# Group-norm attention on one core: GpSimd and VectorE add all eight probability tiles of a head pair, and TensorE counts once

## The chip, the cores and the metric

One core of one Trainium2 chip runs the whole program. The time is the device time of one execution in microseconds (us). The engines are called as in the profile: PE is TensorE, DVE VectorE, ACT ScalarE, POOL GpSimd, SP SyncE, whose queue issues all DMAs here.

## The reference

The input x has shape (16, 192, 32, 32), so 16 images with 192 channels and 1024 positions, all float32. With `_gn` a group norm over 32 groups of 6 channels:

```
xt  = gn(x) as (16, 1024, 192)
qkv = xt @ qkv_w.T                      # 6 heads of 32 channels
attn = softmax((q @ k.T) * 32 ** -0.5)  # 1024 x 1024 for each head
out = (attn @ v) @ proj_w.T + proj_b
x + out
```

## The kernel before, in words

The program runs in steps, one for each image (`b`), and each step in 24 slots (`s`). A slot is one head pair (`PAIRS` = 3) and one tile of 128 keys (`TILES` = 8). Each slot has four units (`u`): two heads of the pair times two halves of 512 queries. The order of everything is written out by hand. Each engine's block has a function `step` that walks through the slots and units, and lists of slots say where the side work stands. Engines wait for each other through counting semaphores. `run_steps` writes out steps -3 to 0, then a loop whose body is two steps, then the last ones. Steps 0 to 15 attend; the earlier ones only prepare.

In a slot, for each unit, PE multiplies keys and queries into a bank of `scores_ps` (L528, two banks), and ACT takes the exponential from there into `probs` (L671), a ring of four tiles. After the second score, PE weighs the slot before: `weigh` (L543) accumulates v times probabilities into `heads_ps`, four column groups, 32 rows each. In parallel PE works on the row maxima of 12 slots later (`row_max`, L453) in three banks of `max_ps`, and DVE reduces them (L812). They become the shift rows, two further rows of `q_stack`.

The denominator of the softmax: POOL adds probability tiles in pairs (L738, two adds of 128x1024 in each odd slot), and PE sums each pair over its 128 keys with a matrix of ones (`count`, L558), which accumulates in `sums_ps`: four counts for each head pair, so 12 a step. ACT copies the sums (L646), SP spreads them, DVE takes the reciprocal (L884), SP writes them through memory and broadcasts them (L394, L397), POOL multiplies the heads (L715) and splits off a low half (L720), and SP moves both halves to `attn_a_hi` and its like (L411).

The side work on PE shares one bank, `extra_ps`, which is freed through `extra_freed`: the products for q and k (`QK_SLOTS`, `QK_LATE_SLOTS`), for v (`V_SLOTS`), the projection (`PROJ_SLOTS`), the transposes for the shift rows (`SHIFT_SLOTS`), the group's mean and variance. q and k are split into a high half by ACT (L601) and a low half by DVE (L865). SP then stacks them with 18 DMAs a step in slots 7, 9 and 11 (`stack_pair`, L359). In slot 13 ACT waits for all of these before it writes `qk_hi` for the next image.

DVE also takes the batch norm statistics in slots 16 and 17 and adds the projection to the residual (L858). The residual `x_res` gets its bias from POOL in slot 9 (L727). POOL computes rstd in slot 2 (L690) and the low halves of the normalised x in slots 8 and 10 (L697, L706).

## Time and profile before

| | us |
|---|---|
| median of the runs (1839.04 to 1847.8) | 1840.49 |
| the profiled execution | 1852.48 |
| its span, first to last instruction | 1850.7 |
| PE busy | 1685.4 |
| ACT busy | 1209.1 |
| DVE busy | 1197.5 |
| POOL busy | 1193.3 |

Busy time counts an engine's instructions, overlaps once. The durations of matmuls overlap, so what one costs in a row of them is read from the distance of the starts. The mean granted clock of PE is 0.951 of 2.4 GHz: it lies at 2.4 GHz with short stretches at 1.2 GHz.

### The profile page before, as it was taken

How to read it: one execution, taken by the hardware profiler on the slowest of the kernel's cores; microseconds unless marked ns; L12 is line 12 of the kernel's file. 1: busy time of each engine (PE TensorE's matmuls, PEld its weight loads, DVE VectorE, ACT ScalarE, POOL GpSimd, SP SyncE). 2: the span in 40 equal slices, each digit the busy share in tenths (PEclk: the TensorE clock that was granted, in tenths of full speed). 3: DMA queues.
4: the chain of work that ended last, by engine and by line, in shares of the span. 5: the costliest groups of instructions: out<-in, count | busy, mean ns of one | idle time of the engine just before them, and what ended most of it. 6: DMA issues, size and time to landing. Idle time of an engine off the chain costs nothing.

```text
span 1850.7 us, 30248 instructions
## 1 busy us (share of the span) xinstructions
PE 1685.4 (91%) x9440; PEld 546.9 (30%) x9440; DVE 1197.5 (65%) x2086; ACT 1209.1 (65%) x1969; POOL 1193.3 (64%) x581
## 2 busy tenths in 40 slices
...
GB/s 68 74 1 81 30 87 42 91 26 54 92 47 87 14 70 75 47 93 48 75 31 71 75 48 87 31 88 39 49 97 48 87 13 84 38 70 53 58 14 80
DMA packets 74284, 109.27 MB, mean 59 GB/s; under 512 B 26176, under 2 KB 39040, under 8 KB 74112
## 3 DMA queue, kind: packets, MB, share of 16 engines
...
q14 instruction: 83, 0.68, 0.1%
...
## 4 chain that ended last, share of the span: by engine, by line
PE 69%; DMA 10%; SPq 9%; ACT 4%; issue 3%; DVE 2%; POOL 1%; ACTq 0%; POOLq 0%; DVEq 0%
PE heads_ps L543 16%; PE max_ps L453 16%; PE scores_ps L528 15%; PE sums_ps L558 9%; SPq L359 7%; DMA k_stack<-qk_lo 7%; ACT probs L671 3%; PE extra_ps L511 2%; DMA inv_rows<-inv_spread 2%; PE extra_ps L512 2%; PE extra_ps L513 2%; PE extra_ps L515 2%; PE extra_ps L516 2%; PE extra_ps L475 1%; PE extra_ps L474 1%
## 5 line engine op out<-in xcount | busy, mean ns | idle before, releaser
L812 DVE TENSOR_REDUCE half_max<-max_ps 128x1 f32<-128x512 f32 x1536 | 1014.8, 686 | 437.6 <-PE max_ps L453 401.9
L671 ACT ACTIVATE probs<-scores_ps,exp_scale 128x512 f32<-128x512 f32 x1536 | 995.8, 688 | 436.7 <-PE scores_ps L528 409.2
L738 POOL TENSOR_TENSOR prob_pairs<-probs 128x1024 f32<-128x1024 f32 x384 | 898.1, 2357 | 511.3 <-ACT probs L671 510.5
L528 PE MATMUL scores_ps<-q_stack,k_stack 98*128 98x512 f16 x1536 | 600.3, 392 | 84.8 <-ACT probs L671 65.8
L453 PE MATMUL max_ps<-k_stack,q_stack 96*128 96x512 f16 x1536 | 607.4, 397 | 7.1 <-DVE half_max L812 4.7
L543 PE MATMUL heads_ps<-probs,v_sb 128*32 128x512 f32 x3072 | 417.4, 616 | 0.1
L453 PEld LDWEIGHTS max_ps<-k_stack,q_stack 96*128 96x128 f16 x1536 | 151.7, 99 | 597.2 <-issue 492.1
L528 PEld LDWEIGHTS scores_ps<-q_stack,k_stack 98*128 98x128 f16 x1536 | 151.8, 99 | 264.6 <-ACT probs L671 181.1
L558 PE MATMUL sums_ps<-prob_pairs,ones 128*32 128x512 f32 x1536 | 215.3, 634 | 1.1 <-POOL prob_pairs L738 1.1
L865 DVE TENSOR_TENSOR qk_lo<-extra_ps,qk_hi 128x512 f16<-128x512 f32 x96 | 66.1, 688 | 107.6 <-ACT qk_hi L601 107.6
L601 ACT CAST qk_hi<-extra_ps 128x512 f16<-128x512 f32 x96 | 55.8, 581 | 95.8 <-DMA k_stack<-qk_lo 58.4
L543 PEld LDWEIGHTS heads_ps<-probs,v_sb 128*32 128x32 f32 x3072 | 60.9, 109 | 144.5 <-issue 133.7
L727 POOL TENSOR_SCALAR x_res<-x_res,bias 96x1024 f32<-96x1024 f32 x32 | 90.7, 2845 | 5.0 <-DMA x_res<-x 4.6
L858 DVE SCALAR_TENSOR_TENSOR x_res<-extra_ps,proj_unscale,x_res 96x512 f32<-96x512 f32 x64 | 46.1, 720 | 48.9 <-PE extra_ps L516 48.9
L626 ACT ACTIVATE xhat<-x_sb,neg_mu_rstd,rstd 128x512 f32<-128x512 f32 x64 | 51.2, 806 | 40.1 <-POOL neg_mu_rstd L693 40.1
L690 POOL TENSOR_TENSOR rstd<-var_eps,minus_half 128x2 f32<-128x2 f32 x16 | 11.5, 716 | 92.3 <-DVE var_eps L849 92.3
L715 POOL TENSOR_TENSOR heads_out<-heads_sb,inv_sb 128x512 f32<-128x512 f32 x48 | 60.8, 1266 | 4.6 <-POOL xhat_b L706 3.5
L720 POOL TENSOR_TENSOR heads_lo<-heads_out,heads_hi 128x512 f16<-128x512 f32 x48 | 55.5, 1156 | 12.1 <-ACT heads_hi L614 12.1
L558 PEld LDWEIGHTS sums_ps<-prob_pairs,ones 128*32 128x32 f32 x1536 | 30.9, 110 | 78.6 <-issue 72.7
L511 PE MATMUL extra_ps<-xhat_a_hi,w_hi 128*128 128x512 f16 x96 | 38.2, 398 | 17.2 <-POOL xhat_b L706 9.4
L614 ACT CAST heads_hi<-heads_out 128x512 f16<-128x512 f32 x48 | 29.6, 617 | 32.3 <-POOL heads_out L715 32.3
L511 PE MATMUL extra_ps<-attn_a_hi,wp_hi 128*96 128x512 f16 x64 | 25.4, 397 | 22.9 <-DMA attn_b<-heads_lo 20.3
...
## 6 DMA issues: line engine op xcount, KB each, us to landing
...
```

What stands on the lines that cost most here:

```text
L359: sp.dma_start(stack[D * n:D * (n + 1), par, 2 * p:2 * p + 2, :], part[row % P:row % P + 2 * D, row // P, :]).then_inc(stacked[p], MOVE)
L453: pe.matmul(max_ps[:, bank, :], q_stack[0:STACK, par, h, P * tile:P * (tile + 1)], k_stack[0:STACK, par, h, HALF * half:HALF * (half + 1)] ...
L511: pe.matmul(to, hi[:, 0, :], a_hi, start=True, stop=False)
L528: pe.matmul(scores_ps[:, u_bank(s, u), :], k_stack[0:SHIFTED, st.parity, h, P * tile:P * (tile + 1)], q_stack[0:SHIFTED, st.parity, h, HAL ...
L543: last = pe.matmul(heads_ps[at:at + D, :], v_sb[:, par, tile, D * h:D * (h + 1)], probs[:, a, s % RING, HALF * half:HALF * (half + 1)], st ...
L558: last = pe.matmul(sums_ps[at:at + D, :], ones[:, 0:D], prob_pairs[:, a, q % PAIR_RING, HALF * half:HALF * (half + 1)], start=(at_pair == ...
L671: nc.scalar.activation(probs[:, a, s % RING, HALF * half:HALF * (half + 1)], scores_ps[:, u_bank(s, u), :], ACT.Exp, scale=exp_scale[:, 0: ...
L715: nc.gpsimd.tensor_tensor(heads_out[:, :], heads_sb[:, (par + p) % 2, :], inv_sb[:, :], ALU.mult).then_inc(divided, 1)
L727: nc.gpsimd.tensor_scalar(x_res[:, t, :], x_res[:, t, :], bias[:, t:t + 1], None, ALU.add).then_inc(res_biased, 1)
L738: nc.gpsimd.tensor_tensor(prob_pairs[:, a, j % PAIR_RING, :], probs[:, a, (s - 1) % RING, :], probs[:, a, s % RING, :], ALU.add).then_inc( ...
L812: nc.vector.tensor_reduce(half_max[:, a, tile, half:half + 1], max_ps[:, bank, :], AX_X, ALU.max).then_inc(max_read[bank], 1)
L865: nc.vector.tensor_tensor(qk_lo[:, t, n], extra_ps[:, :], qk_hi[:, t, n], ALU.subtract).then_inc(extra_freed, 1)
```

## The change

The banks: `sums_ps` is gone and `scores_ps` has a third bank. The exponentials of units 0 to 2 go to `probs`, now a ring of six tiles with 1536 columns. Those of unit 3 go to `probs_last`, eight tiles with 512 columns.

The sums: POOL no longer adds in pairs. In each slot but the first of a head pair it adds the tile to `prob_sums`, in two instructions of 1024 and 512 columns. DVE sums unit 3: in slots 4 and 8 after a pair's start, after units 1 and 3, it reduces four tiles at a time over 256 columns (`sum_quads`). The first four go into `prob_sums`, the second four into `quad_sums`. POOL adds these two at the next pair's first slot. PE then sums each pair once over its keys, into `extra_ps`, in slots 10, 18 and 2 of the next step (`SUMS_SLOTS`). ACT copies it out at the next slot's start.

The bias of the residual moves from POOL to ACT, in slots 10 and 11. Mean and variance go from slots 0 and 2 to 0 and 1, with rstd in slot 2 still. One q and k product goes from slot 16 to 15, two projections from 17 and 18 to 16 and 17. Spreading, reciprocal, broadcasting, dividing, and moving the heads of pairs 1 and 2 stand one slot earlier.

```diff
-SCORE_BANKS = 2
+SCORE_BANKS = 3
 MAX_BANKS = 3
 MAX_UNITS = SCORE_UNITS * SLOTS // MAX_BANKS
-RING = 4
-PAIR_RING = 4
+RING = 6
+QUAD = 4
+WIDE = 3 * HALF
+ADDED = 2 * (TILES - 1) + 1
+QUADS = 4
...
-MEAN_SLOT, VAR_SLOT = 0, 2
+MEAN_SLOT, VAR_SLOT = 0, 1
+RSTD_SLOT = 2
...
-QK_SLOTS = (12, 16, 19)
+QK_SLOTS = (12, 15, 19)
 QK_LATE_SLOTS = (3, 4, 6)
-PROJ_SLOTS = (17, 18, 20, 22)
-EXTRA_SLOTS = (*SHIFT_SLOTS, MEAN_SLOT, VAR_SLOT, *V_SLOTS, *QK_SLOTS, *QK_LATE_SLOTS, *PROJ_SLOTS)
+PROJ_SLOTS = (16, 17, 20, 22)
+SUMS_SLOTS = {10: 0, 18: 1, 2: 2}
...
-BIAS_SLOT = 9
+BIAS_AT = ((10, 1), (11, 3))
...
 HEADS_TAKEN = TILES
-SUMS_TAKEN = TILES + 4
-SUMS_SPREAD = TILES + 5
-INVERTED = TILES + 6
-INV_SPREAD = TILES + 7
-DIVIDED = TILES + 11
-MOVED = (23, 22, 22)
-COUNT_UNIT, HEADS_UNIT, SUMS_UNIT = 3, 2, 3
+SUMS_SPREAD = TILES + 4
+INVERTED = TILES + 5
+INV_SPREAD = TILES + 6
+DIVIDED = TILES + 10
+MOVED = (23, 21, 21)
+HEADS_UNIT = 2
...
-        sums_ps = psum("sums_ps", [P, HALF])
...
-        probs = sb("probs", [P, 2, RING, N], F32)
-        prob_pairs = sb("prob_pairs", [P, 2, PAIR_RING, N], F32)
+        probs = sb("probs", [P, RING, WIDE], F32)
+        probs_last = sb("probs_last", [P, 2 * QUAD, HALF], F32)
+        prob_sums = sb("prob_sums", [P, 2, 2 * N], F32)
+        quad_sums = sb("quad_sums", [P, HALF], F32)
...
-                        sp.wait_ge(sums_taken, k + 1)
+                        sp.wait_ge(extra_freed, st.ordinal(s - 2) + 1)
...
+                elif kind == "sums" and part == 0:
+                    j, par = st.summed(i)
+                    pe.wait_ge(tiles_added, ADDED * (PAIRS * j + i + 1))
+                    for half in range(HALVES):
+                        for a in range(2):
+                            at, u = D * (2 * half + a), 2 * a + half
+                            last = pe.matmul(extra_ps[at:at + D, :], ones[:, 0:D],
+                                             prob_sums[:, (par + i) % 2, HALF * u:HALF * (u + 1)],
+                                             start=True, stop=True)
...
-            def count(b, q):
-                p, at_pair = divmod(q, PAIRS_A_HEAD)
-                pe.wait_ge(pairs_added, 2 * (SLOTS // PAIR * b + q + 1))
-                if at_pair == 0 and due(PAIRS * b + p):
-                    pe.wait_ge(sums_taken, PAIRS * b + p)
-                for half in range(HALVES):
-                    for a in range(2):
-                        at = D * (2 * half + a)
-                        last = pe.matmul(sums_ps[at:at + D, :], ones[:, 0:D],
-                                         prob_pairs[:, a, q % PAIR_RING, HALF * half:HALF * (half + 1)],
-                                         start=(at_pair == 0), stop=(at_pair == PAIRS_A_HEAD - 1))
-                last.then_inc(sums_done, 1)
...
+                elif kind == "sums":
+                    k = PAIRS * st.summed(i)[0] + i
+                    if due(k):
+                        act.wait_ge(sums_spread_out, MOVE * k)
+                    nc.scalar.copy(sums_sb[:, :], extra_ps[:, :]).then_inc(extra_freed, 1)
+            def add_bias(st, t):
+                if t == 0:
+                    act.wait_ge(res_loaded, MOVE * st.b)
+                nc.scalar.activation(x_res[:, t, :], x_res[:, t, :], ACT.Identity,
+                                     bias=bias[:, t:t + 1]).then_inc(res_biased, 1)
...
+                                was, tile = divmod(s - RING, TILES)
                                 act.wait_ge(heads_done, SLOTS * st.b + s - RING + 1)
-                                act.wait_ge(pairs_added, 2 * (SLOTS // 2 * st.b + (s - RING) // 2 + 1))
+                                act.wait_ge(tiles_added, ADDED * (PAIRS * st.b + was) + 2 * max(tile, 1))
+                            k = PAIRS * st.b + s // TILES
+                            if u == 3 and s % QUAD == 0 and due(k):
+                                act.wait_ge(quads_summed, QUADS * (k - 1) + 2 * (s % TILES // QUAD + 1))
...
-                    if st.tail and s == BIAS_SLOT:
-                        pool.wait_ge(res_loaded, MOVE * st.b)
-                        pool.sem_inc(res_seen, 1)
-                        for t in range(2):
-                            nc.gpsimd.tensor_scalar(x_res[:, t, :], x_res[:, t, :], bias[:, t:t + 1], None,
-                                                    ALU.add).then_inc(res_biased, 1)
-                    if st.attend and s % 2 == 1:
-                        j = s // 2
-                        for a in range(2):
-                            pool.wait_ge(probs_ready, SCORE_UNITS * (SLOTS * st.b + s) + 2 * (a + 1))
-                            counted = SLOTS // PAIR * st.b + j - PAIR_RING + 1
-                            if a == 0 and due(counted):
-                                pool.wait_ge(sums_done, counted)
-                            nc.gpsimd.tensor_tensor(prob_pairs[:, a, j % PAIR_RING, :],
-                                                    probs[:, a, (s - 1) % RING, :],
-                                                    probs[:, a, s % RING, :], ALU.add).then_inc(pairs_added, 1)
+                    for j, par, p in st.due(s, TILES, TILES):
+                        k = PAIRS * j + p
+                        last = prob_sums[:, (par + p) % 2, WIDE:WIDE + HALF]
+                        pool.wait_ge(quads_summed, QUADS * (k + 1))
+                        nc.gpsimd.tensor_tensor(last, last, quad_sums[:, :], ALU.add).then_inc(tiles_added, 1)
+                    if st.attend and s % TILES != 0:
+                        p, tile = divmod(s, TILES)
+                        k = PAIRS * st.b + p
+                        for n, cols in enumerate((slice(0, N), slice(N, WIDE))):
+                            to = prob_sums[:, (st.parity + p) % 2, cols]
+                            pool.wait_ge(probs_ready, SCORE_UNITS * (SLOTS * st.b + s) + n + 2)
+                            if tile == 1:
+                                if n == 0 and due(k - 1):
+                                    pool.wait_ge(extra_filled, st.ordinal(TILES * p))
+                                before = probs[:, (s - 1) % RING, cols]
+                            else:
+                                pool.wait_ge(tiles_added, ADDED * k + 2 * (tile - 2) + n + 1)
+                                before = to
+                            nc.gpsimd.tensor_tensor(to, before, probs[:, s % RING, cols],
+                                                    ALU.add).then_inc(tiles_added, 1)
...
+            def sum_quads(st, s, u):
+                for g in range(2):
+                    for j, par, p in st.due(s, QUAD * (g + 1), TILES):
+                        k = PAIRS * j + p
+                        n = slice(N // 4 * (u // 2), N // 4 * (u // 2 + 1))
+                        if u == 1:
+                            dve.wait_ge(probs_ready, SCORE_UNITS * (SLOTS * j + TILES * p + QUAD * (g + 1)))
+                            if g == 0 and due(k - 1):
+                                dve.wait_ge(extra_filled, st.ordinal(TILES * p))
+                            if g == 1 and due(k):
+                                dve.wait_ge(tiles_added, ADDED * k)
+                        to = quad_sums[:, n] if g == 1 else prob_sums[:, (par + p) % 2, WIDE:WIDE + HALF][:, n]
+                        nc.vector.tensor_reduce(to, probs_last[:, QUAD * g:QUAD * (g + 1), n].rearrange("p t n -> p n t"),
+                                                AX_X, ALU.add).then_inc(quads_summed, 1)
...
+def tile_of(probs, probs_last, s, u):
+    return probs_last[:, s % (2 * QUAD), :] if u == 3 else probs[:, s % RING, HALF * u:HALF * (u + 1)]
```

On POOL, in the loop, from slot 8 of a step on, before the change. `prob_pairs` takes two tiles, and two adds stand for each two slots:

```order
L696 REGISTER_ALU
L697 TENSOR_TENSOR xhat_a_lo<-xhat,xhat_a_hi 128x1024 [waits xhat_ready]
L724 REGISTER_ALU
L727 TENSOR_SCALAR x_res<-x_res,bias 96x1024 [waits res_loaded]
L727 TENSOR_SCALAR x_res<-x_res,bias 96x1024
L733 ISA
L737 REGISTER_ALU [waits probs_ready]
L738 TENSOR_TENSOR prob_pairs<-probs 128x1024 [waits sums_done]
L733 REGISTER_ALU
L738 TENSOR_TENSOR prob_pairs<-probs 128x1024 [waits probs_ready]
```

The same engine and place after the change. `prob_sums` is the running sum, L735 the last add of a pair, and L751 the add of a tile, here the first of a pair:

```order
L703 REGISTER_ALU
L704 TENSOR_TENSOR xhat_a_lo<-xhat,xhat_a_hi 128x1024 [waits xhat_ready]
L734 ISA
L735 TENSOR_TENSOR prob_sums<-prob_sums,quad_sums 128x512 [waits quads_summed]
L742 ISA
L746 REGISTER_ALU [waits probs_ready]
L751 TENSOR_TENSOR prob_sums<-probs 128x1024 [waits extra_filled]
L742 REGISTER_ALU
L751 TENSOR_TENSOR prob_sums<-probs 128x512 [waits probs_ready]
```

The bias is gone from between the low half of x-hat and the adds, and in its place stands the last add, which waits for DVE's `quads_summed`.

On DVE, in the loop, slot 16 before the change, with two of the four statistics (`half_stats`):

```order
L812 TENSOR_REDUCE half_max<-max_ps 128x1 [waits max_filled1]
L788 ISA
L789 BN_STATS half_stats<-x_sb 128x6 [waits x_loaded]
L812 TENSOR_REDUCE half_max<-max_ps 128x1 [waits max_filled2]
L808 REGISTER_ALU
L812 TENSOR_REDUCE half_max<-max_ps 128x1 [waits max_filled0]
L789 BN_STATS half_stats<-x_sb 128x6
L812 TENSOR_REDUCE half_max<-max_ps 128x1 [waits max_filled1]
```

The same engine and slot after the change:

```order
L824 TENSOR_REDUCE half_max<-max_ps 128x1 [waits max_filled1]
L800 ISA
L801 BN_STATS half_stats<-x_sb 128x6 [waits x_loaded]
L824 TENSOR_REDUCE half_max<-max_ps 128x1 [waits max_filled2]
L834 ISA
L839 REGISTER_ALU [waits probs_ready]
L841 TENSOR_REDUCE quad_sums<-probs_last 128x256 [waits tiles_added]
L820 REGISTER_ALU
L824 TENSOR_REDUCE half_max<-max_ps 128x1 [waits max_filled0]
L801 BN_STATS half_stats<-x_sb 128x6
L824 TENSOR_REDUCE half_max<-max_ps 128x1 [waits max_filled1]
L841 TENSOR_REDUCE quad_sums<-probs_last 128x256
```

Two reduces over `probs_last` now stand among the four maxima and the statistics; the first waits for the last add that POOL makes for the pair before.

On PE, in the loop, in slot 13 before the change, a count behind unit 3's score (such a one stands in each odd slot):

```order
L527 REGISTER_ALU
L528 MATMUL scores_ps<-q_stack,k_stack 128x512 [waits probs_ready]
L552 ISA
L558 MATMUL sums_ps<-prob_pairs,ones 32x512 [waits sums_taken,pairs_added]
L558 MATMUL sums_ps<-prob_pairs,ones 32x512 x3
L453 MATMUL max_ps<-k_stack,q_stack 128x512 [waits max_read2]
```

The same engine after the change, in slot 10, one of the three slots with a count:

```order
L557 MATMUL heads_ps<-probs,v_sb 32x512 [waits probs_ready]
L557 MATMUL heads_ps<-probs,v_sb 32x512 x2
L557 MATMUL heads_ps<-probs_last,v_sb 32x512
L468 REGISTER_ALU
L512 REGISTER_ALU [waits extra_freed]
L516 MATMUL extra_ps<-prob_sums,ones 32x512 [waits tiles_added]
L516 MATMUL extra_ps<-prob_sums,ones 32x512 x3
L458 MATMUL max_ps<-k_stack,q_stack 128x512 [waits max_read2]
```

The sums matmul waits for POOL's `tiles_added` in the place right behind the weighing, with the row maxima behind it, and it fills the shared bank `extra_ps`.

## Rows read from the trace of the kernel before

**Rows 1.** The page, part 1: busy us, share of the span, instructions of each engine.
```profile
PE 1685.4 (91%) x9440; PEld 546.9 (30%) x9440; DVE 1197.5 (65%) x2086; ACT 1209.1 (65%) x1969; POOL 1193.3 (64%) x581
```

**Rows 2.** Busy us by stretch: us, engines with instruction counts, PEclk, DMA share, GB/s.
```profile
853.00:1064.00 211.00, 199.39 (x1140) 65.47 (x1137) 143.69 (x251) 146.15 (x239) 143.22 (x71) 0.96 0.30 64
```

**Rows 3.** The waits, whole span: engine and line, awaited; us, times, longest.
```profile
POOL prob_pairs L738 <- ACT probs L671: 510.5, 154, 40.3
...
ACT probs L671 <- PE scores_ps L528: 409.2, 654, 4.1
...
PE scores_ps L528 <- ACT probs L671: 65.8, 27, 6.2
...
ACT qk_hi L601 <- DMA k_stack<-qk_lo: 58.4, 12, 6.3
```

**Rows 4.** Timeline of POOL: start us, us; the step's rstd, ten steps apart.
```profile
443.81 0.72 POOL L690 TENSOR_TENSOR rstd<-var_eps,minus_half 128x2 f32<-128x2 f32 x1 [3.19 <-DVE var_eps L849]
...
1542.15 0.72 POOL L690 TENSOR_TENSOR rstd<-var_eps,minus_half 128x2 f32<-128x2 f32 x1 [2.85 <-DVE var_eps L849]
```

**Rows 5.** Timeline of PE at full clock: a weighing, a count, their neighbours.
```profile
1048.48 1.06 PE L543 MATMUL heads_ps<-probs,v_sb 128*32 128x512 f32 x8
1049.48 0.39 PE L453 MATMUL max_ps<-k_stack,q_stack 96*128 96x512 f16 x1
1049.70 0.38 PE L528 MATMUL scores_ps<-q_stack,k_stack 98*128 98x512 f16 x1
...
1050.14 0.38 PE L528 MATMUL scores_ps<-q_stack,k_stack 98*128 98x512 f16 x1
1050.45 1.07 PE L558 MATMUL sums_ps<-prob_pairs,ones 128*32 128x512 f32 x8
1051.45 0.39 PE L453 MATMUL max_ps<-k_stack,q_stack 96*128 96x512 f16 x1
```

**Rows 6.** Timeline of PE: the loop's end (869.75) and slot 13's stall (1039.52).
```profile
869.75 0.39 PE L528 MATMUL scores_ps<-q_stack,k_stack 98*128 98x512 f16 x1 [2.21 <-issue]
...
872.25 0.61 PE L453 MATMUL max_ps<-k_stack,q_stack 96*128 96x512 f16 x1
...
1039.52 0.61 PE L528 MATMUL scores_ps<-q_stack,k_stack 98*128 98x512 f16 x1 [5.58 <-ACT probs L671]
```

**Rows 7.** Groups by line: shapes, count, busy us, mean ns, idle before.
```profile
L812 DVE TENSOR_REDUCE half_max<-max_ps 128x1 f32<-128x512 f32 x1536 | 1014.8, 686 | 437.6 <-PE max_ps L453 401.9 <-issue 21.8 <-DVE shift_rows L829 9.1
...
L671 ACT ACTIVATE probs<-scores_ps,exp_scale 128x512 f32<-128x512 f32 x1536 | 995.8, 688 | 436.7 <-PE scores_ps L528 409.2 <-PE heads_ps L543 9.6 <-issue 9.0
...
L727 POOL TENSOR_SCALAR x_res<-x_res,bias 96x1024 f32<-96x1024 f32 x32 | 90.7, 2845 | 5.0 <-DMA x_res<-x 4.6
...
L715 POOL TENSOR_TENSOR heads_out<-heads_sb,inv_sb 128x512 f32<-128x512 f32 x48 | 60.8, 1266 | 4.6 <-POOL xhat_b L706 3.5 <-DMA inv_sb<-inv_rows 0.9
...
L720 POOL TENSOR_TENSOR heads_lo<-heads_out,heads_hi 128x512 f16<-128x512 f32 x48 | 55.5, 1156 | 12.1 <-ACT heads_hi L614 12.1
...
L697 POOL TENSOR_TENSOR xhat_a_lo<-xhat,xhat_a_hi 128x1024 f16<-128x1024 f32 x16 | 34.0, 2124 | 6.1 <-ACT xhat_a_hi L626 6.1
...
L757 DVE TENSOR_REDUCE l_max<-max_ps 128x1 f32<-128x192 f32 x1 | 0.3, 348 | 0.0
```

**Rows 8.** Timeline of POOL and DVE: merged runs of equal instructions.
```profile
898.15 4.68 POOL L738 TENSOR_TENSOR prob_pairs<-probs 128x1024 f32<-128x1024 f32 x2 [2.56 <-ACT probs L671]
...
918.37 2.48 DVE L812 TENSOR_REDUCE half_max<-max_ps 128x1 f32<-128x512 f32 x4 [0.68 <-PE max_ps L453]
```

**Rows 9.** The chain that ended last, slots 7 to 12 of one step.
```profile
905.06 0.70 DVE qk_lo L865
...
909.63 3.11 DMA inv_rows<-inv_spread
...
923.56 8.79 DMA k_stack<-qk_lo
```

**Rows 10.** The waits of SP's queue, whole span.
```profile
SPq L411 <- POOL heads_lo L720: 7.3, 1, 7.3
```

56 lines of the change are left out of this document (26 added, 30 removed).

## The prediction, made before the changed kernel was run

> **What bounds the kernel now.** I read the busy shares first [rows 1]: PE 91%, DVE, ACT and POOL 64 to 65% each. The stretch of 211 us in the middle of the loop [rows 2] shows the same: PE busy for 199.39 of 211 us, the others for 143 to 146, at a granted clock of 0.96. Then the waits [rows 3]: POOL waits 510.5 us for probabilities and ACT 409.2 for scores. Both wait for work that TensorE paces. So TensorE's instruction stream sets the time, and the others have slack.
>
> A step (one image, 24 slots) takes (1542.15 - 443.81) / 10 = 109.8 us [rows 4]. There are 16 attending steps. Before them lies a prologue that ends near 115 us, which the change leaves as it is.
>
> What a slot costs on PE is read from starts, since the durations overlap [rows 5]: a row max and a score product follow each other by 0.22 us. The weighing matmuls (x8) start at 1048.48, and the next row max at 1049.48: 1.00 us. The count starts at 1050.45, 0.31 after the score product ahead of it, and the next row max at 1051.45. Where only a row max follows a score it comes after 0.22, so one count costs 1.00 + 0.09 = 1.09 us. A plain slot has 8 products and one weighing, 7 x 0.22 + 0.31 + 1.00 = 2.85 us.
>
> Two things of the old step are not matmul work [rows 6]. First, once per iteration of two steps PE fetches for 2.21 us at the loop's end and then runs at half the clock (row max 0.61 instead of 0.38). Second, in slot 13 ACT waits for the stack DMAs of this step before it may overwrite qk_hi, 58.4 us in 12 times [rows 3]. PE then stands for 5.58 us and starts again at half the clock [rows 6]. The chain to that wait is shown in [rows 9]: the last qk_lo at 905.06, six DMA issues, the wait for inv_rows (3.11 us from 909.63), more issues, the last DMA from 923.56 for 8.79 us, to 932.35. That is 27.3 us for slots 7 to 12, and ACT goes on after it.
>
> **The change part by part.**
>
> *Counts off TensorE.* 12 counts a step become 3: 9 x 1.09 = 9.8 us less on PE, and this lies on the path. Alone it gives a step of 109.8 - 9.8 = 100.0 us. Everything below corrects that number.
>
> *GpSimd.* Out go 24 adds of 128x1024 (two in 4.68 us, so 2.34 each [rows 8]) and two bias adds (2.845 each [rows 7]): 61.8 us. In come 21 x (2.34 for 1024 columns + 1.20 for 512), the 512 taken between heads_lo's 1.156 and heads_out's 1.266 [rows 7], and three last adds at 1.20: 74.3 + 3.6 = 77.9 us. With what stays (3 x 2.42 for heads_out and heads_lo, 2.12 each for the two x-hat remainders [rows 7], about 0.9 for the group norm, of which rstd is 0.72 [rows 4]) POOL has 77.9 + 7.3 + 4.2 + 0.9 = 90.3 us a step. That is under 100, so it is no bound on average, but it is 90% full, and in order. By octets of slots: slots 0 to 7 need 29 us, 8 to 15 need 33 (both x-hat remainders lie there), 16 to 23 need 28. PE has some 29, 28 and 28 us of work there. The new wait stands in PE's queue: in slots 10, 18 and 2 the sums matmul waits for tiles_added, and behind it is everything PE has. For slot 10 POOL has to do slots 1 to 7 and then xhat_a_lo and the last add of slot 8, about 31.5 us. PE comes from slot 1 to slot 10 in about 29.5 us less ACT's lag of half a slot. So I expect 2 to 4 us of standing there. Much of it falls within slots 7 to 12, which the stack chain holds in any case, so I book 1.5 us a step. Bounds: 0, and 5 if POOL's backlog also reaches slots 18 and 2.
>
> *VectorE.* In come 12 reduces a step, 128x256 out of 1024 elements, read with four tiles innermost (a hop of 512 words at each element). No row of before has such a hop. Their contiguous price: 128x192 takes 348 ns and 128x512 takes 686 [rows 7], 1.06 ns an element, so 686 + 512 x 1.06 = 1.23 us, and 1.13 where they follow something (four back to back take 2.48 us, so each 0.60 [rows 8], plus 0.54). If each hop cost a second cycle it would be 2.2 us. I take 1.2, as the nearest row, and keep 2.2 for the rivals. DVE's sum: 1197.5 / 16 = 74.8 busy a step [rows 1], plus 12 x 1.2 = 89 us. Again under 100, but bunched: slot 16 holds two reduces, two statistics, one qk_lo and four maxima, 2.4 + 0.6 + 1.3 + 0.6 + 2.3, about 6.6 us [rows 7, 8] against some 3.9 of PE (a plain slot and one projection). Only three max banks lie between, about 2 us of PE, and in slot 17 the projection waits for DVE to free extra_ps. That costs PE about 1.5 us in 16 and 17, and a few tenths in each of 0, 4, 8, 12 and 20 (DVE 4.7 to 5.6 us, PE 2.9 to 3.9). I book 2.5 us a step. Bounds: 0 and 6 (at 1.85 us a reduce).
>
> The Trainium skill, Vector Engine (DVE) Microarchitecture Reference, "The SBUF access granule: adjacent pairs" (the paragraph of that name), speaks against this part: a port streams at full rate only over runs of adjacent words, and one source that hops at each element is given as 1.73 ns a column. By that an estimate for a reduce is 1024 x 1.73, about 1.8 us. The same paragraph tells of a one-source read that hopped and ran at full rate. No row of before can tell the two apart; the second rival is this case.
>
> *ScalarE.* In come two bias activations of 96x1024; the sums copy stays. With 688 ns for 512 columns [rows 7] that is at most 2 x 1.4 = 2.8 us on 1209/16 = 75.6 [rows 1]: 78 of 100 us, beside PE's work, 0 on the path. If ACT were the one waited for it would be 2.8.
>
> *Third score bank.* PE may be one score further ahead. Its idle time for probabilities is 65.8 us in all [rows 3], nearly all of it the stack stall, and the weighing still waits for all four tiles of the slot before. I book -1.0 a step (bounds 0 and -3, the gaps hidden in overlapped durations).
>
> *Places moved.* The sums of a pair go out one slot earlier, so in slot 6 instead of 7 SP waits for inv_rows: 3.11 us plus an issue of 0.60 leave the stack chain, 27.3 becomes 23.6. PE's own work in slots 7 to 12 falls by three counts less one, 2.2 us. So the stall shrinks somewhat further than PE's work does: -0.5. Bounds: -1.5 where all 3.7 us come out, and +3 if SP is held in slot 5 by a late heads_lo, as POOL is now full; behind it the shift rows and the stacks are queued.
>
> **The sum.** 100.0 + 1.5 + 2.5 + 0 - 1.0 - 0.5 = 102.5 us a step; 7.3 less in each of 16, 117 us. The profiled execution took 1852.48 us (span 1850.7), so 1735.5; the median of the runs shown stands to it as 1840.49 to 1852.48, 0.65% less: **1724 us**.
>
> **The rivals.**
>
> *1. The stalls dissolve (better).* Half-clock stretches and the stack stall give POOL and DVE time to catch up; the terms of 1.5 and 2.5 vanish and the banks give 1.5: 98.5 a step, 181 us less, 1671 by the profile, 1660 us. For it: both stay under 91 us of work. Against it: bunching in the slots named.
>
> *2. The reduces hop (DVE becomes the bound).* At 1.85 us DVE has 97 us of busy time, and its stall grows from 2.5 to 6: 106 a step, 61 us less, 1791, so 1780 us. For it: the hop of 2 KB. Against it: one input and one output for four reads.
>
> *3. Slower: DVE past the old step.* One mechanism: if a reduce takes 2.5 us, DVE has 74.8 + 30 = 105 us and stands for some 2 x 2.5 in each of six slots with only three max banks between. Its stall then is 6 + 12 x 0.65 = 14 in place of 2.5: 114 a step, 67 us more, 1919, so 1907 us. It decides from about 2.15 us a reduce, where the stall passes 9.8 us. For it: half rate gives 2.2 already. Against it: no row shows such a rate.
>
> *4. The coupling over SP.* POOL late with heads_lo holds SP, and the stack chain and slot 13 slip: +5, 107.5 a step, 37 us less, 1816, so 1804 us. Against it: SP waited for heads_lo once, for 7.3 us [rows 10].
>
> That the counts don't leave PE can be ruled out by the order of the instructions.
>
> **How the numbers follow.** Forecast 0.48 (1690 to 1755), rival 1 0.16, rival 2 0.18, rival 4 0.07, rival 3 0.11. The range goes from 1655 to 1805: it takes in rivals 1, 2 and 4 and leaves out rival 3 and some of the rest. A measurement of this kernel can tell about 0.5% from no change. Faster 0.86, same 0.03, slower 0.11: the slower case is rival 3, and the same is the ground between it and rivals 2 and 4.
>
> **What would show it.** Steps of 102 to 103 us between the group norm's rstd instructions. POOL busy 85 to 90% in the loop, PE about 90% and lower in sum by 16 x 9.8 = 157 us. Reduces near 1.2 us; at 1.8 rival 2 holds, above 2.15 rival 3. PE waiting for POOL at the sums matmul by 1 to 4 us in slot 10 and nearly not in 18 and 2. PE waiting for DVE in slots 16 and 17. ACT's wait for the stack DMAs shorter than the 58.4 us in all. It would be wrong if adds in place took longer than 2.34 and 1.20 us, as 10% there makes POOL the bound at 98 us, or if the half-clock stretches grew with PE's new idle time.

## The result: slower by a tenth, and the profile after

The changed kernel takes **2039.6 us** (median, 2032.52 to 2054.66), against 1841.3 us for the kernel before in the same comparison: a ratio of **1.108, 95% interval 1.1045 to 1.1115**. The forecast was 1724 us with a range of 1655 to 1805, so the time lies far outside, on the other side of no change. The profiled execution has a span of 2030.7 us, to be held against 1850.7. It is the shortest of its four, and the one before was longer than the others of its kernel, so the spans differ by 180 us and the medians by 198.

The page of the changed kernel, busy us of each engine (to be read against [rows 1]) and, from its second part, the granted clock of TensorE in 40 slices:

```profile
PE 1665.1 (82%) x8288; PEld 564.1 (28%) x8288; DVE 1562.8 (77%) x2278; ACT 1228.3 (60%) x2001; POOL 1461.3 (72%) x885
...
PEclk9989898887988889797998879889798897999895
```

The matmuls fell from 9440 to 8288, as the change says; their busy time fell by 20 us only, where 9 counts of 1.09 us in 16 steps are 157. The instructions that stayed ran slower: the mean granted clock of the span is 0.875, against 0.951 before. The rows show two levels, a matmul of 512 columns at 0.38 to 0.39 us (2.4 GHz) or at 0.60 to 0.63 us (1.2 GHz), with single ones between where the level changes, so 2 x (1 - 0.875) x 2030.7 = 508 us were run at the half, against 2 x (1 - 0.951) x 1850.7 = 181 us. And PE's idle time grew from 165 to 366 us. The same in the middle of the loop, to be read against [rows 2]:

```profile
853.00:1064.00 211.00, 179.91 (x908) 60.78 (x907) 171.57 (x251) 134.90 (x221) 160.48 (x97) 0.87 0.23 54
```

Steps between rstd instructions on POOL, as in [rows 4]: (1684.49 - 478.68) / 10 = 120.6 us in place of 109.8. Sixteen times 10.8 is 173 of the 180 us by which the span grew, so the loss is in the steps:

```profile
478.68 0.70 POOL L697 TENSOR_TENSOR rstd<-var_eps,minus_half 128x2 f32<-128x2 f32 x1 [3.24 <-DVE var_eps L878]
...
1684.49 0.70 POOL L697 TENSOR_TENSOR rstd<-var_eps,minus_half 128x2 f32<-128x2 f32 x1 [3.31 <-DVE var_eps L878]
```

What PE waits for is in the list of waits (engine and line, awaited; us, times, longest):

```profile
PE extra_ps L472 <- DVE qk_lo L894: 67.8, 29, 2.5
...
PE extra_ps L479 <- DVE chan_var L874: 53.9, 15, 5.1
...
PE max_ps L458 <- DVE half_max L824: 49.0, 40, 2.7
...
PE extra_ps L525 <- DVE x_res L887: 43.3, 17, 3.0
...
PE extra_ps L472 <- DVE x_res L887: 34.8, 14, 2.5
```

All five name VectorE, 248.8 us together, and they are stalls that come back in each step, none over 5.1 us. Four stand behind the new reduces; the second, chan_var, is another matter, shown below. None of them stood in the old list at that size; its largest was ACT's probabilities, 65.8 us [rows 3]. The reduces are the new work on VectorE (groups by line: shapes, count, busy us, mean ns, idle before):

```profile
L841 DVE TENSOR_REDUCE prob_sums<-probs_last 128x256 f32<-128x1024 f32 x96 | 186.0, 1939 | 7.4 <-ACT probs_last L678 7.4
L841 DVE TENSOR_REDUCE quad_sums<-probs_last 128x256 f32<-128x1024 f32 x96 | 184.0, 1918 | 8.4 <-ACT probs_last L678 8.4
```

One takes 1.93 us, not the 1.2 that the forecast took: rival 2's duration, and a little over it. The timeline shows how it reaches PE. VectorE in slot 16 (start us, us):

```profile
904.71 0.67 DVE L824 TENSOR_REDUCE half_max<-max_ps 128x1 f32<-128x512 f32 x1
905.30 1.95 DVE L841 TENSOR_REDUCE quad_sums<-probs_last 128x256 f32<-128x1024 f32 x1
907.17 0.68 DVE L824 TENSOR_REDUCE half_max<-max_ps 128x1 f32<-128x512 f32 x1
907.76 0.68 DVE L801 BATCH_NORM_STATS2 half_stats<-x_sb 128x6 f32<-128x512 f32 x1
908.36 0.68 DVE L824 TENSOR_REDUCE half_max<-max_ps 128x1 f32<-128x512 f32 x1
908.95 1.88 DVE L841 TENSOR_REDUCE quad_sums<-probs_last 128x256 f32<-128x1024 f32 x1
910.75 0.74 DVE L887 SCALAR_TENSOR_TENSOR x_res<-extra_ps,proj_unscale,x_res 96x512 f32<-96x512 f32 x1
```

And PE at the same place:

```profile
908.13 0.38 PE L542 MATMUL scores_ps<-q_stack,k_stack 98*128 98x512 f16 x1
911.54 0.66 PE L525 MATMUL extra_ps<-attn_a_hi,wp_hi 128*96 128x512 f16 x1 [3.03 <-DVE x_res L887]
...
912.85 0.63 PE L458 MATMUL max_ps<-k_stack,q_stack 96*128 96x512 f16 x1
```

VectorE has not one gap in it (its rows run on without one from 902.31 to 913.28): two reduces stand ahead of the x_res of the last projection, which frees extra_ps. PE's next projection waits 3.03 us for it, and goes on at half the clock (a row max 0.63 us, 0.39 at full). A step has five or six such places, of 1.8 to 3.0 us. The half clock does not follow each of them: after the 2.22 us at 893.59 the row maxima stay at 0.39.

One place has a second cause. In slot 0 VectorE works out the group's variance in two operations of 128x2, each with both inputs in SBUF, and PE's next product waits for the second. Beside GpSimd's adds they look so:

```profile
955.54 1.26 DVE L871 TENSOR_TENSOR mu_off<-mu_off 128x2 f32<-128x2 f32 x1
956.84 2.26 DVE L874 TENSOR_TENSOR chan_var<-chan_stats,mu_off 128x2 f32<-128x2 f32 x1
...
955.52 1.27 POOL L735 TENSOR_TENSOR prob_sums<-prob_sums,quad_sums 128x512 f32<-128x512 f32 x1 [11.28 <-DVE quad_sums L841]
956.75 3.56 POOL L751 TENSOR_TENSOR prob_sums<-probs 128x1024 f32<-128x1024 f32 x2
...
959.16 0.58 PE L479 MATMUL extra_ps<-chan_var,mean_a 128*128 128x1 f32 x2 [2.19 <-DVE chan_var L874]
```

In the kernel before, where GpSimd is idle at that point, the same two take 0.16 us each:

```profile
877.25 0.16 DVE L842 TENSOR_TENSOR mu_off<-mu_off 128x2 f32<-128x2 f32 x1
877.45 0.16 DVE L845 TENSOR_TENSOR chan_var<-chan_stats,mu_off 128x2 f32<-128x2 f32 x1
```

The first ends at 956.80, as GpSimd's add of 512 columns does (956.79), and the second at 959.10, 2.35 us after GpSimd's add of 1024 columns began, which is what such an add takes (the row of 3.56 us is that add and one of 512). So the rows show VectorE held for the length of GpSimd's adds. Two parts of the change make this a stall: the new last add starts when the reduces end, right beside the two operations, and the variance's product stands in slot 1 where it stood in slot 2.

In the window 853 to 1064 the idle PE rows over 0.3 us add up to 30.7 us, and to 10.7 in the kernel before.

### The profile page after: what moved, and what is told of

Its sections match the earlier page's. It is cut to its first block, busy times and chain, and to the rows that moved or that the text cites. A ratio compares the mean times of both kernels' runs of the same rounds, so it can differ in the third digit from the quotient of the medians.

```text
span 2030.7 us, 29328 instructions
## 1 busy us (share of the span) xinstructions
PE 1665.1 (82%) x8288; PEld 564.1 (28%) x8288; DVE 1562.8 (77%) x2278; ACT 1228.3 (60%) x2001; POOL 1461.3 (72%) x885
## 4 chain that ended last, share of the span: by engine, by line
PE 49%; DVE 26%; issue 16%; POOL 4%; ACT 3%; DMA 1%; SPq 1%; DVEq 0%; ACTq 0%; POOLq 0%
PE heads_ps L557 13%; PE max_ps L458 12%; PE scores_ps L542 10%; DVE half_max L824 9%; DVE prob_sums L841 5%; DVE quad_sums L841 5%; POOL prob_sums L751 3%; PE extra_ps L516 2%; DVE qk_lo L894 2%; PE extra_ps L525 2%; DVE chan_var L874 1%; PE extra_ps L526 1%; PE extra_ps L480 1%; ACT probs_last L678 1%; PE extra_ps L479 1%
## 5 line engine op out<-in xcount | busy, mean ns | idle before, releaser
L751 POOL TENSOR_TENSOR prob_sums<-prob_sums,probs 128x1024 f32<-128x1024 f32 x576 | 1029.0, 1815 | 151.8 <-ACT probs L678 151.3
L678 ACT ACTIVATE probs<-scores_ps,exp_scale 128x512 f32<-128x512 f32 x1152 | 755.9, 694 | 362.0 <-PE scores_ps L542 353.9
L542 PE MATMUL scores_ps<-q_stack,k_stack 98*128 98x512 f16 x1536 | 634.5, 415 | 21.0 <-issue 17.3
L557 PE MATMUL heads_ps<-probs,v_sb 128*32 128x512 f32 x2304 | 467.7, 688 | 8.0 <-ACT probs_last L678 5.0
L557 PE MATMUL heads_ps<-probs_last,v_sb 128*32 128x512 f32 x768 | 462.6, 688 | 0.0
L678 ACT ACTIVATE probs_last<-scores_ps,exp_scale 128x512 f32<-128x512 f32 x384 | 264.5, 689 | 305.5 <-PE scores_ps L542 302.7
L735 POOL TENSOR_TENSOR prob_sums<-prob_sums,quad_sums 128x512 f32<-128x512 f32 x48 | 60.6, 1263 | 237.8 <-DVE quad_sums L841 237.8
L751 POOL TENSOR_TENSOR prob_sums<-probs 128x1024 f32<-128x1024 f32 x96 | 171.5, 1806 | 37.0 <-ACT probs L678 37.0
L841 DVE TENSOR_REDUCE prob_sums<-probs_last 128x256 f32<-128x1024 f32 x96 | 186.0, 1939 | 7.4 <-ACT probs_last L678 7.4
L841 DVE TENSOR_REDUCE quad_sums<-probs_last 128x256 f32<-128x1024 f32 x96 | 184.0, 1918 | 8.4 <-ACT probs_last L678 8.4
```

The lines of the kernel that those rows point to most:

```text
L542: pe.matmul(scores_ps[:, u_bank(s, u), :], k_stack[0:SHIFTED, st.parity, h, P * tile:P * (tile + 1)], q_stack[0:SHIFTED, st.parity, h, HAL ...
L557: last = pe.matmul(heads_ps[at:at + D, :], v_sb[:, par, tile, D * h:D * (h + 1)], tile_of(probs, probs_last, s, 2 * a + half), start=(tile ...
L678: nc.scalar.activation(tile_of(probs, probs_last, s, u), scores_ps[:, u_bank(s, u), :], ACT.Exp, scale=exp_scale[:, 0:1]).then_inc(probs_r ...
L735: nc.gpsimd.tensor_tensor(last, last, quad_sums[:, :], ALU.add).then_inc(tiles_added, 1)
L751: nc.gpsimd.tensor_tensor(to, before, probs[:, s % RING, cols], ALU.add).then_inc(tiles_added, 1)
L841: nc.vector.tensor_reduce(to, probs_last[:, QUAD * g:QUAD * (g + 1), n].rearrange("p t n -> p n t"), AX_X, ALU.add).then_inc(quads_summed, 1)
```

## The experiments

The theory after the traces: the reduces alone make the loss, by their duration, through VectorE's lag; the other parts do about what was forecast. Rivals: the length of GpSimd's adds, the third bank, the one bank `extra_ps` that all side work shares, and that PE's clock falls because the counts are gone. Whether VectorE and GpSimd hold each other up at SBUF is seen in the rows above and in the kernels with adds in place of reduces.

**Reduces at the contiguous price.** The same count and size of reduces, but each reads four adjacent words for one output, so the sums that it takes are not the softmax's:

```diff
-nc.vector.tensor_reduce(to, probs_last[:, QUAD * g:QUAD * (g + 1), n].rearrange("p t n -> p n t"),
-                        AX_X, ALU.add).then_inc(quads_summed, 1)
+h = QUAD * g + QUAD // 2 * (u // 2)
+flat = probs_last[:, h:h + 2, :].rearrange("p t (m q) -> p (t m) q", q=QUAD)
+nc.vector.tensor_reduce(to, flat, AX_X, ALU.add).then_inc(quads_summed, 1)
```

> The changed kernel, but each reduce on VectorE reads its 1024 elements in address order (four neighbours for each output) in place of a hop of 512 words at each element. The sums of the fourth unit come out wrong; all the waits, counts and shapes are the same. Theory D (the reduces stand in VectorE's queue ahead of what frees extra_ps, and TensorE waits there; their length is the price): the reduces fall from 1.93 to about 1.2 us, the stalls of 2.2 to 5.4 us in seven slots of a step shrink by 0.7 to 1.4 us each and the clock's half-rate stretches with them: 2030.7 us of span become about 1860 to 1900. Rival P (GpSimd's 91 us a step with its waits sets the pace): the time stays within 2% of 2030.7, and the waits move to the sums matmul.

Measured 1828.5 us, ratio 0.990 (0.987 to 0.9934), span 1826.7. Page and group:

```profile
PE 1562.6 (86%) x8288; PEld 541.0 (30%) x8288; DVE 1418.2 (78%) x2278; ACT 1218.3 (67%) x2001; POOL 1460.1 (80%) x885
...
L843 DVE TENSOR_REDUCE quad_sums<-probs_last 128x256 f32<-128x1024 f32 x96 | 115.9, 1209 | 8.4 <-ACT probs_last L678 8.4
```

1209 ns is the forecast's 1.2 us. So the hop is worth 0.72 us a reduce and 211 us in all, more than theory D expected (1860 to 1900 for the span). But even without it the change gains 1%, not 6: the duration was only part of the mistake.

**Reduces of four columns.** The same instructions and waits, nearly no work; most sums are left out:

```diff
+few = slice(n.start, n.start + 4)
-nc.vector.tensor_reduce(to, probs_last[:, QUAD * g:QUAD * (g + 1), n].rearrange("p t n -> p n t"),
+nc.vector.tensor_reduce(to[:, 0:4], probs_last[:, QUAD * g:QUAD * (g + 1), few].rearrange("p t n -> p n t"),
```

> The changed kernel with VectorE's 192 reduces cut to four columns each, the rest of the fourth unit's sums being left out (its columns keep ones from a memset at the start). GpSimd's and TensorE's work is all there. Theory D: what is left is the change as meant, TensorE less nine counts a step: about 102 us a step, a span of 1700 to 1750. Rival P: GpSimd alone holds the pace, 1850 or more. Between the two, about 1800, lies a share for each.

Measured 1725.9 us, ratio 0.935 (0.9318 to 0.9385), span 1724.7, inside theory D's range.

```profile
PE 1536.2 (89%) x8288; PEld 545.8 (32%) x8288; DVE 1246.1 (72%) x2280; ACT 1213.5 (70%) x2001; POOL 1457.7 (85%) x885
```

This kernel has the matmuls, the adds on GpSimd, the biases and the banks of the changed one. Against it the changed kernel's span is 306 us longer: 128.9 of PE busy with the same 8288 matmuls (the clock) and 177.1 of PE idle (the stalls). All of this loss hangs on the time that the reduces take on VectorE. The rival of GpSimd's adds is out as its cause, since they are all here (POOL 1457.7 us). What is left here of the stall at chan_var:

```profile
PE extra_ps L479 <- DVE chan_var L877: 30.3, 15, 5.9
```

It was 1.5 us in the kernel before.

**Two score banks again.** `SCORE_BANKS = 3` back to 2, nothing else.

> The changed kernel with two score banks in place of three, nothing else. Theory D: TensorE hardly waits for probabilities in the changed kernel, so the third bank is worth 0 to 1.5% (2030.7 to 2060). Rival: the third bank does harm or carries much of the load, over 2% either way.

Measured 2051.3 us, ratio 1.112 (1.1089 to 1.1154), span 2039.8. That is 9 us more by the spans and 12 by the medians, 0.4 to 0.6%; the intervals overlap, so a small gain from the third bank is likely and not settled, as theory D has it, and an effect of over 1% either way is out.

**The counts put back as idle work.** Two score banks, and 9 times a step the four matmuls of 512 columns of a count into a bank that nothing reads; this is work beyond what the kernel needs. The source is `ones` read four times over, since SBUF has no room for a tile of its own:

```diff
+if u == 3 and st.attend and s % 2 == 1 and s % TILES != 3:
+    for n in range(4):
+        pe.matmul(idle_ps[D * n:D * (n + 1), :]..., ones[:, 0:D], ones[:, :]..., start=True, stop=True)
```

> The changed kernel with two score banks and, in nine odd slots of a step, four matmuls of a count's shape on constant data into the bank that is then free: TensorE has as much work as in the kernel before, 9.8 us a step or 157 us in all, and nobody waits for it. Beside the run with two banks alone (span 2039.8). Theory D (VectorE's queue sets the pace in most slots): at most a third of the 157 us shows, under 50 us. Rival T (TensorE is the bound and its stalls merely add): the time rises by 130 to 157 us.

Measured 2142.2 us, ratio 1.163 (1.1563 to 1.1688), span 2139.8. That is 91 us above the run with two banks (100 by the spans) for 157 us of matmuls: between what the two theories expected. Taking the counts off TensorE thus bought some 60% of its price here; the rest lay beside stalls that stayed. Full cover by the stalls is out, and so is a pure TensorE bound. The clock is 0.911 with them and 0.889 without, where it was 0.951 before the change: the want of the counts makes about a third of its fall, the rest comes with the stalls.

**The reduces alone, in the kernel before.** To the kernel before come 12 reduces of the same shape a step, at the same slots, of constants, whose result nothing uses (hop of 32 words):

```diff
+if u % 2 == 1 and s % 4 == 0 and (st.attend and s > 0 or st.tail and s == 0):
+    four = ones[:, :].rearrange("p (t n) -> p n t", t=4).unsqueeze(1).broadcast_to([P, 8, 32, 4])
+    nc.vector.tensor_reduce(idle_sum[:, :, :], four, AX_X, ALU.add).then_inc(idle_step, 1)
```

> The kernel before, whole, plus 12 reduces a step on VectorE in slots 4, 8, 12, 16, 20 and 0 of the next, 1024 elements with a hop of 32 words at each, whose result nobody reads. No count leaves TensorE. Theory D: their place in the queue costs here too, near what it costs in the changed kernel against the tiny reduces (311 us), less what the longer slots hide: 1850 becomes 1980 to 2120. Rival: with TensorE as the bound they are hidden, under 1900. If a hop of 32 words is read at full rate (1.2 us), about 1900 to 1930.

Measured 2097.2 us, ratio 1.138 (1.1274 to 1.1483), span 2107.2.

```profile
L886 DVE TENSOR_REDUCE idle_sum<-ones 128x256 f32<-128x1024 f32 x192 | 371.8, 1937 | 0.1
```

So 23.2 us of VectorE work a step, put where the change puts it, cost (2097.2 - 1841.3) / 16 = 16 us a step in a kernel whose VectorE was 65% busy [rows 1]. This is inside what theory D expected, and the rival that a TensorE bound hides the reduces is out. All else in the change is then worth 58 us (2097.2 to 2039.6) with the reduces there and 115 (1841.3 to 1725.9) with hardly any.

**Half of the reduces moved to emptier slots.** The reduces of a pair's first four tiles go to slots 7, 14 and 23:

```diff
+first = {7: 0, 14: 1, 23: 2}
-    for j, par, p in st.due(s, QUAD * (g + 1), TILES):
+    at = st.due(s, 2 * QUAD, TILES) if g else [(st.b, st.parity, first[s])] if st.attend and s in first else []
+    for j, par, p in at:
```

> The changed kernel with the first two reduces of each pair in slots 7, 14 and 23 in place of 4, 12 and 20: the slots behind these wait for extra_ps from ScalarE or not at all, while in 5, 13 and 21 TensorE waited 2.5 to 2.9 us for a qk_lo or x_res that stood behind the reduces. Same number and length of reduces. Theory D1 (what counts is that they stand ahead of what frees extra_ps): three stalls of 2.5 us in 16 steps go, and a part of the half-clock time: 2030.7 becomes 1890 to 1930. Rival D2 (what counts is VectorE's work in a short stretch, with three max banks): slots 7 and 8 now hold four reduces in a row, and the time stays within 2% of 2030.7.

Measured 1962.1 us, ratio 1.065 (1.0593 to 1.0701): 77 us back, with VectorE's work the same. That is between the two theories (1890 to 1930, and within 2% of 2030.7), so each has a part. The waits for extra_ps at the shift transposes are gone from the head of the list, and this one has taken their place:

```profile
PE max_ps L458 <- DVE half_max L824: 122.7, 146, 2.6
```

**The shift transposes into a bank of their own.** On the kernel with two score banks, so that they need not wait for VectorE to free extra_ps:

```diff
-if part == 0 and due(g):
+if part == 0 and due(g) and kind != "shift":
     pe.wait_ge(extra_freed, g)
-last = pe.transpose(extra_ps[0:2 * TILES, 0:P], neg_max[:, :], ident[:, :])
+last = pe.transpose(shift_ps[0:2 * TILES, 0:P], neg_max[:, :], ident[:, :])
```

> The changed kernel with two score banks, and the bank that is then free given to the transposes for the shift rows, which no longer wait for extra_ps in slots 5, 13 and 21, where they waited 2.2 to 2.9 us behind a qk_lo or x_res. The reduces stand where they stood, with the same length. Beside the run with two banks alone (span 2039.8). Theory S (the shared bank turns VectorE's lag into waits): 3 x 2.5 us in 16 steps and part of the half-clock time go, 1880 to 1940. Rival M (VectorE's lag is passed on by whatever comes next, the three max banks): as with the moved reduces, the wait moves to the row maxima, and it stays at 1990 to 2045.

Measured 2050.6 us, ratio 1.115 (1.1129 to 1.1169), against 1.112 for the same kernel without the bank: no gain, as rival M said (its bound of 2045 is passed by 2 us of span). In the list of waits:

```profile
PE max_ps L459 <- DVE half_max L825: 143.8, 80, 2.8
```

Idle rows of PE in the window 853 to 1064 sum to 30.7 us, against 30.6 in the kernel with two banks, and the stalls of one step at the three transposes' places are 2.45, 1.76 and 2.50 where they were 2.49, 1.78 and 2.54. The lag is VectorE's; the next bank that VectorE frees, here a row maximum's, collects it. So the rival that extra_ps is too narrow a gate has fallen for the transposes; the wait of the projection for extra_ps (3.03 us) was not tested so.

**Interleaved tiles, so that the reduces read adjacent words.** probs_last as [P, 2, HALF, QUAD]; three score banks, and the same sums as the changed kernel:

```diff
-probs_last = sb("probs_last", [P, 2 * QUAD, HALF], F32)
+probs_last = sb("probs_last", [P, 2, HALF, QUAD], F32)
-return probs_last[:, s % (2 * QUAD), :] if u == 3 else ...
+return probs_last[:, s % (2 * QUAD) // QUAD, :, s % QUAD] if u == 3 else ...
```

> The changed kernel with the fourth unit's four tiles of a quad interleaved in memory: ScalarE writes them and TensorE reads them with a hop of four words, and VectorE's reduces read in address order. The result is the reference's. Theory D: as in the contiguous run, reduces of about 1.2 us and 1828 us, plus what the hops cost on the other two engines. If both take them at full rate, 1825 to 1840; if TensorE reads the hop at half rate, a fourth of the weighing takes 0.2 to 0.9 us more in each of 384 slots, and 1900 to 2100 come out.

Measured 2088.8 us, ratio 1.133 (1.1286 to 1.1381), span 2090.6, inside the expected 1900 to 2100. The groups:

```profile
L557 PE MATMUL heads_ps<-probs_last,v_sb 128*32 128x512 f32 x768 | 778.0, 1102 | 0.0
...
L678 ACT ACTIVATE probs_last<-scores_ps,exp_scale 128x512 f32<-128x512 f32 x384 | 453.5, 1181 | 124.9 <-PE scores_ps L542 123.9 <-DVE quad_sums L841 0.8
...
L557 PE MATMUL heads_ps<-probs,v_sb 128*32 128x512 f32 x2304 | 423.9, 628 | 82.9 <-ACT probs_last L678 82.7
...
L841 DVE TENSOR_REDUCE quad_sums<-probs_last 128x256 f32<-128x1024 f32 x96 | 115.9, 1209 | 13.7 <-ACT probs_last L678 13.7
```

The reduces are cheap, and the hop has moved to the others: TensorE reads a moving operand with it at 1102 ns against 628, ScalarE writes with it at 1181 against 682 for its `probs` tiles. PE is busy for 1877.5 us, 315 more than with the same reduces read contiguously, and is the bound again.

**No reduces: VectorE adds tile by tile.** GpSimd adds the first 1536 columns of each tile as in the change, VectorE the last 512, both in place in SBUF:

```diff
-nc.vector.tensor_reduce(to, probs_last[...], AX_X, ALU.add).then_inc(quads_summed, 1)
+nc.vector.tensor_tensor(to, before, probs[:, at % RING, WIDE:2 * N], ALU.add).then_inc(units_added, 1)
```

> The changed kernel with VectorE adding the fourth unit tile by tile, one tensor_tensor of 128x512 in each slot with a tile to add (336 in all), in place of 192 reduces of four tiles; GpSimd's last add falls away. VectorE's work is about 336 x 0.7 = 235 us in place of 370 us, and at most one such stands in a slot. Theory D with even placing: near the run with tiny reduces, 1740 to 1800. Rival L (both engines' adds of two SBUF tensors exclude each other, as the Trainium skill says of the shared port pair): an add waits for up to one GpSimd add of 2.3 us, its duration in the trace rises above 1.5 us, and the time is 1850 to 2100.

Measured 1831.1 us, ratio 0.994 (0.9903 to 0.9971); the profiled execution, with a span of 1842.2, is the longest of ten. The time lies between the two theories (1740 to 1800, and 1850 to 2100), and an add at 1.44 us is a little under rival L's 1.5. The groups:

```profile
L837 DVE TENSOR_TENSOR prob_sums<-prob_sums,probs 128x512 f32<-128x512 f32 x288 | 413.3, 1435 | 10.0 <-ACT probs L676 9.7
...
L743 POOL TENSOR_TENSOR prob_sums<-prob_sums,probs 128x1024 f32<-128x1024 f32 x576 | 1144.3, 2015 | 47.7 <-ACT probs L676 47.4
```

An add of 512 columns takes 1.44 us where one of this size with an operand in PSUM takes 0.69 (below), and GpSimd's mean add rose from 1815 to 2015 ns. Nearly all of that is in its adds of 512 columns (1274 to 1616 ns; those of 1024 go from 2357 to 2415). The two slow each other down. The Trainium skill, SBUF — State Buffer, "Who interferes with whom", says that a VectorE instruction with two inputs in SBUF contends with a GpSimd instruction that reads SBUF; the rows agree.

**The same adds with the running sum in PSUM.** Two score banks; the freed one holds the sum, and only the last add of a pair writes to SBUF:

```diff
+unit_ps = psum("unit_ps", [P, HALF])
-to = prob_sums[:, (par + p) % 2, WIDE:2 * N]
+to = prob_sums[:, (par + p) % 2, WIDE:2 * N] if tile == TILES - 1 else unit_ps[:, :]
-    before = to
+    before = unit_ps[:, :]
```

> As the run with adds on VectorE, but the running sum of the fourth unit lies in the PSUM bank that the third score bank had (so two score banks), and goes to SBUF with the last tile. Six of seven adds then have one SBUF input in place of two. Rival L was borne out by 1.435 us an add: if that was the shared port, six in seven adds fall to 0.7 us, VectorE loses some 200 us of busy time and GpSimd's adds are back at 2.35 and 1.27 us; 1740 to 1790 us. If the length came from the port for other reasons (in place, or the reading of fresh data), it stays near 1831, plus up to 1% for the bank.

Measured **1722.2 us, ratio 0.936 (0.9301 to 0.9417)**, span 1705.1 at a clock of 0.97. It beats both kernels. It is also below the 1740 to 1790 that was expected. Page and groups:

```profile
PE 1529.6 (90%) x8288; PEld 529.0 (31%) x8288; DVE 1389.6 (81%) x2422; ACT 1221.0 (72%) x2001; POOL 1414.4 (83%) x837
...
L840 DVE TENSOR_TENSOR unit_ps<-unit_ps,probs 128x512 f32<-128x512 f32 x240 | 165.3, 689 | 11.1 <-ACT probs L677 11.1
L840 DVE TENSOR_TENSOR unit_ps<-probs 128x512 f32<-128x512 f32 x48 | 77.3, 1610 | 0.0
L840 DVE TENSOR_TENSOR prob_sums<-unit_ps,probs 128x512 f32<-128x512 f32 x48 | 32.7, 681 | 4.4 <-POOL prob_sums L744 2.4 <-ACT probs L677 2.0
```

Only the first add of a pair still reads two SBUF tiles, and it alone is dear: 1610 ns against 689. GpSimd's adds are back at 2358 and 1310 ns. The reduces' 370 us have become 275, in pieces of 0.69 us, one a slot, and the half clock lasts 2 x 0.03 x 1705 = 102 us in place of 508. GpSimd's last add is gone here too, and with it the stall at chan_var: that operation takes 0.16 us again and PE waits 1.5 us for it in all. No run tells this part of the gain from that of the reduces.

**The add ahead of the row max.** In the same kernel, the two lines changed places:

```diff
-if st.maxed(s) is not None:
-    row_max(st, s, u)
 if u == 1:
     add_unit(st, s)
+if st.maxed(s) is not None:
+    row_max(st, s, u)
```

> The same with VectorE's add ahead of the second unit's row maximum in place of behind it, where VectorE waits for TensorE's weighing (1.0 us). Theory: 0.7 us a slot fit into that wait, and it is 0 to 2% faster than the one beside it; never slower than 0.5%, as the tile it adds is done before the weighing starts.

Measured 1742.2 us, ratio 0.943 (0.9375 to 0.949). A miss: a gain of 0 to 2% was expected and at most 0.5% of loss, and the median is 1.2% higher. The intervals overlap, so that it loses is likely and not settled; the adds with two SBUF inputs take 1973 ns there.

**GpSimd alone.** The kernel before with the biases on ScalarE; GpSimd also adds the pairs to quads, and TensorE counts 6 times a step in place of 12:

```diff
+if j % 2 == 1:
+    for a in range(2):
+        nc.gpsimd.tensor_tensor(prob_pairs[:, a, j % PAIR_RING, :], prob_pairs[:, a, (j - 1) % PAIR_RING, :],
+                                prob_pairs[:, a, j % PAIR_RING, :], ALU.add).then_inc(quads_added, 1)
```

> The kernel before with the bias on ScalarE and GpSimd adding two pairs to a quad (two further adds of 128x1024 in every second odd slot), so that TensorE counts six times a step in place of twelve; VectorE's work is as before. TensorE loses 6 x 1.09 = 6.5 us a step, GpSimd has 74.6 - 5.7 + 28.1 = 97 us. If GpSimd keeps pace: 103 to 105 us a step and 1735 to 1770 us. If its full queue delays the release of probability tiles (a ring of four): 1780 to 1850.

Measured 1846.6 us, ratio 1.000 (0.9965 to 1.003), span 1852.2, as expected for a full queue, with 6 x 16 x 1.09 = 105 us of counts gone. PE's busy time fell by 56 (1628.9; the clock is 0.927 against 0.951), its idle time rose by 58. The waits:

```profile
PE scores_ps L528 <- ACT probs L679: 90.4, 62, 5.8
...
PE max_ps L453 <- DVE half_max L822: 34.6, 19, 8.3
```

The first was 65.8 in 27 times [rows 3]. GpSimd, 83% busy, adds in runs of four at 2.36 us; that its lag holds the ring of probabilities is argued from this row, not tested.

## Why the prediction was wrong, by its own steps

**Counts off TensorE, -9.8: right as work.** With hardly any reduces PE is busy for 149 us less, against 157 by the sum. In the changed kernel itself putting the work back cost about 60% of it.

**GpSimd, +1.5: work right, stall too high.** It was forecast at 1193.3 + 16 x 16.1 = 1451 us of busy time and has 1461.3; adds of 1024 and 512 columns average 1815 ns as (2.35 + 1.27) / 2. The sums matmul waits for it 11.6 us in all, 9.1 of them once, where 24 were booked. That the stalls gave GpSimd time has its share in this; in the kernel with tiny reduces it is 18.8 us, again 9.1 of them once. What the term left out is that GpSimd's adds hold up VectorE, which is the stall at chan_var.

**ScalarE, 0, and third bank, -1.0: right within what can be told.** ACT has 1228.3 us (forecast at most 1254); the bank brought 9 to 12 us, 0.6 to 0.8 a step, if it brought anything.

**Places moved, -0.5: right for the stacks, and one place was left out.** The wait of ACT for the stack DMAs, 58.4 us before [rows 3], has no row in the list of after, where the longer step hides it; in the kernel with tiny reduces it is 28.3 us. But the variance's product, moved from slot 2 to slot 1, was booked at nothing, and it is where PE stands for chan_var: 30.3 us with tiny reduces, 1.8 a step more than before.

Without VectorE's term the sum gave 100.0 a step, 157 us less; the kernel with tiny reduces is 115 us faster by the medians, 126 by the spans. So 31 to 42 us, 2 to 2.6 a step, are missing. By the spans 8 of them are PE's busy time and 23 its idle time, in which the other terms came to 0. In its list of waits the stack stall falls by more than was booked (65.8 us before, 22.3 now, under the name qk_lo); against it stand chan_var (30.3 for 1.5), the sums matmul (18.8), the fetch at the loop's end ("issue", 18.6 for 10.6) and the weighing's wait for ACT (9.6).

**VectorE, +2.5: this step failed,** and it carries nearly the whole miss. Of the 316 us between 1724 and 2039.6, the reduces' 314, less the 40 booked for them, are 274; the 42 just named are the rest. The step had three faults, each with its run:

1. *The duration.* "I take 1.2, as the nearest row". It is 1.93. At 1.21 us the kernel takes 1828.5, so this is 211 of the 314 us above the tiny reduces. The nearest row had no hop in it. The Trainium skill's rule that I weighed there (Vector Engine (DVE) Microarchitecture Reference, "The SBUF access granule: adjacent pairs"), one source that hops at each element, gave an estimate of 1.8 us: the trace sides with it, a little above.
2. *The price of a lag.* At 1.21 us the reduces cost (1828.5 - 1725.9) / 16 = 6.4 us a step where 2.5 stood, and at 1.93 they cost 19.6 where the upper bound was 6. From one to the other PE loses 13.2 us a step for 8.7 us of VectorE work. I compared VectorE's load with PE's slot by slot, and took the 2 us between max banks as slack in each. But around each pair of reduces VectorE runs 7 to 11 us without a gap, over some three slots, and this slack is there once for all of them. Then it idles, while PE, held up, gives it nothing; behind the reduces of slot 8:

```profile
880.63 2.48 DVE L824 TENSOR_REDUCE half_max<-max_ps 128x1 f32<-128x512 f32 x4 [2.55 <-PE max_ps L458]
```

Each step so has five or six stalls of 2 to 3 us, not one. The run with a bank of its own for the transposes shows that a stall taken away at one place can come back whole at the next bank; with moved reduces 77 us of it stayed away. The sums of busy time (98 of 120 us) said nothing on that. (The forecast's sum for slot 16 prints a term of 0.6 too many; its total, 6.6 us, is right for the instructions named.)

3. *The clock.* Nothing was booked for it beyond a last sentence. After most of the stalls PE's rows are at half the clock; of the 306 us over the tiny reduces, 129 are longer busy time of the same matmuls.

**The rivals.** Rival 2 had the right duration and the wrong price: 106 us a step where 120.6 came. It took 3.5 us for 0.65 us more of each of 12 reduces, while rival 3 took 8 for the same; by rival 3's own rate the price would have been 110.3, no gain. Rival 3 is what happened in kind, VectorE past the old step, but it was put at 2.15 us a reduce and up. Between 1.21 us (ratio 0.990) and 1.93 us (1.108), a straight line crosses 1 at about 1.27 us. Rival 1 did not occur (its own terms add up to 98.0 a step and not 98.5, which changes nothing here). Rival 4's wait did: SP waits for heads_lo 207.9 us in 32 times, against once before [rows 10]. It costs nothing that shows in the changed kernel, since PE waits for stack DMAs 2.2 us in all, and ACT not at all.

That 1724 us is nearly what the kernel with tiny reduces (1726) and the one with the sum in PSUM (1722) take is chance in part: the first falls 2 to 2.6 us a step short of its terms, which the 2.5 for VectorE happens to equal.
